# The RMS factor taken from the layer norm's variance, with memsets, routing steps, filler products and gathers re-placed, in an image tower with mixture-of-experts on one core

## The chip, the core and the metric

The kernel runs on one NeuronCore of a Trainium2 chip, with everything in float32. The metric is device time in microseconds: the median of several executions of one launch. Engine names are those of the profile: PE is TensorE (PEld its weight loads), DVE VectorE, ACT ScalarE, POOL GpSimd, SP SyncE.

## What is computed

32 images are cut into 25 patches each and embedded; with the class token that is 26 tokens of 192 numbers per image, 832 in all. Then come a first causal attention (12 heads of 16), and a block of a second causal attention (12 query heads of 64 on 3 key heads, with rotary turns) and 16 experts of which each token uses 2. Cut to what matters for the change:

```python
def _layernorm(x, eps=1e-5):
    m, v = mean(x), var(x)
    return (x - m) / sqrt(v + eps)

def rms_norm(x, w):                       # EPS = 1e-6
    return x / sqrt(mean(x * x) + EPS) * w

h = tok(x, W, b)                          # patches, bias, position; class token in front
h = h + attn1(_layernorm(h))
z = _layernorm(h)                         # input of the block, and its residual
x2 = z + attention2(rms_norm(z, norm1_w))
h = h + x2 + moe(rms_norm(x2, norm2_w))   # router, softmax, top 2 of 16, silu(gate) * up, down
```

`z` has mean 0 and mean square v / (v + 1e-5). So the factor of the first `rms_norm` can be had from v alone: (h - m) times 1 / sqrt(v (1 + 1e-6) + 1e-6 * 1e-5).

## The kernel before

**Tiles and stages.** A tile holds 4 images (32 rows each, 26 used), a group two tiles; there are 4 groups. Each group goes through stage A (patches, first attention, residual `h`, layer norm `z`, product input `u`) and stage B (second attention, `x2`, norm, router logits), in eight phases each, `a1` to `a8` and `b1` to `b8`. The function `stages` sets the order by hand, the same for all engines: two stages run as a pair, phase by phase. The pairs are A0 with A1, B0 with A2, B1 with A3, B2 with B3. Every engine executes its part of each phase in that order, and the engines meet by semaphores. The routing steps of the first four tiles (`choose`, `ranks`, `place`, `scatter`) are hung into the last pair, after the phase of B2 that the last argument of `stages` names; those of the other four tiles follow the pair.

**End of stage A (`a8`).** DVE adds the projection to the residual (L893), takes mean and variance of the rows (`layer_stats`: L799, L803), adds epsilon (L806). POOL raises to -0.5 (`rstd`, L516). DVE writes `zB` (`normalise`, L811). ACT squares it and sums (`squares`, L674), DVE scales the sum (`mean_square`, L818), POOL raises again (L516), DVE writes `u` (L899). PE transposes `u` (`turned`, L1089), ACT copies the result out of the bank with the norm's weight (L689).

**Start of stage B.** PE makes value products (L1216) and rotary ones (L1228); DVE multiplies those by the turn table (L912), POOL adds the halves (L555) and spreads the keys (L560). PE may make the fourth rotary set when DVE has read the first, since they share a bank. POOL's `pads` zeroes four buffers (L507 to L510) in `b1` of groups 0 and 3.

**Filler.** `keep_busy` (L1100) issues products that nobody reads ahead of a wait of PE.

**End of stage B.** Output products (L1286) give `x2` on DVE (L948), ACT squares it (L674), DVE scales (L818), POOL raises (L516) and adds the residual (L570), DVE writes `u` (L951), SP stores it as the experts' input, PE transposes it and makes the logits (L1301).

**Routing.** `choose` (L974 to L987) takes the two best experts, `place` (L994 to L1013) numbers the slots, and POOL's `scatter` writes 4 tiles times 2 choices into the slot table by eight indirect DMAs (L580). After the last of all 16, SP reads 28 tile entries one after the other (L462), and after these issues the later half of the late expert weights (L358).

**Experts.** A tile of 128 slots is gathered (L596), transposed (L1328), multiplied by one expert's gate and up weights (L1333), gated (L762, L1053), transposed (L1341), multiplied by the down weights (L1350), scaled (L1057) and scattered to its token's row (L602). Between 13 and 28 tiles can be used; POOL runs 8 gathers ahead, and each `step` issues one scatter and one gather. At the end both parts and the residual are added and stored.

## Time and profile before

| | us |
|---|---|
| median of 3 runs (336.48 to 338.42) | 337.66 |
| the profiled execution | 340.81 |
| its span | 338.9 |
| busy: PE | 274.5 (81%) |
| busy: DVE | 149.4 (44%) |
| busy: POOL | 123.8 (37%) |
| busy: ACT | 91.5 (27%) |

The mean granted clock of TensorE was 0.934 of full speed. A tenths digit of the page stands for 8.5 us of the span. PE's busy time holds filler products: 376 recorded rows of L1100, 48.4 us. Each matmul of the program shows as two recorded rows (20 rotary products of a group are x40 in the trace). A wait is put down to the event that came last; the busy shares are means over stages with different limits.

### The profile page before, as it was taken

How to read it: one execution, taken by the hardware profiler on the slowest of the kernel's cores; microseconds unless marked ns; L12 is line 12 of the kernel's file. 1: busy time of each engine (PE TensorE's matmuls, PEld its weight loads, DVE VectorE, ACT ScalarE, POOL GpSimd, SP SyncE). 2: the span in 40 equal slices, each digit the busy share in tenths (PEclk: the TensorE clock that was granted, in tenths of full speed). 3: DMA queues.
4: the chain of work that ended last, by engine and by line, in shares of the span. 5: the costliest groups of instructions: out<-in, count | busy, mean ns of one | idle time of the engine just before them, and what ended most of it. 6: DMA issues, size and time to landing. Idle time of an engine off the chain costs nothing.

```text
span 338.9 us, 5708 instructions
## 1 busy us (share of the span) xinstructions
PE 274.5 (81%) x1917; PEld 232.9 (69%) x1917; DVE 149.4 (44%) x347; ACT 91.5 (27%) x248; POOL 123.8 (37%) x138
## 2 busy tenths in 40 slices
PE   1999889979889999698999779803899999999900
PEld 0988779868768889487998669703677776777600
DVE  0143845764744568733867843570022222222204
ACT  1016640204532216512100532100233333333200
POOL 5030002573001291011794056063334523666640
PEclk9999999959999999999999999755899999999965
DMA  7301992004500007000000000392111596222226
GB/s 297 156 2 43 390 314 71 2 0 140 140 0 21 0 2 186 2 5 17 1 2 0 3 1 21 96 343 76 37 35 39 163 281 169 72 70 58 62 72 219
DMA packets 16641, 30.56 MB, mean 90 GB/s; under 512 B 6500, under 2 KB 10820, under 8 KB 15780
## 3 DMA queue, kind: packets, MB, share of 16 engines
q1 hardware_dynamic: 11140, 20.43, 20.1%
q0 software_dynamic: 2720, 4.55, 4.8%
q10 hardware_dynamic: 2752, 5.18, 4.5%
q8 instruction: 20, 0.33, 0.4%
q14 instruction: 9, 0.07, 0.1%
HBM read 26.07 MB, written 4.09 MB: 89 GB/s over the span
## 4 chain that ended last, share of the span: by engine, by line
PE 31%; DVE 21%; issue 16%; POOL 14%; DMA 11%; ACT 6%; SPq 0%; POOLq 0%; DVEq 0%; ACTq 0%
PE bank L1228 8%; POOL front L596 4%; POOL slots L580 4%; DMA experts<-wgu 4%; POOL parts L602 3%; PE bank L1244 3%; PE bank L1286 2%; PE bank L1333 2%; POOL rstd_a L516 2%; PE bank L1112 2%; DVE experts L835 2%; DMA front<-fw 2%; DVE experts L951 2%; DMA front<-moe_in,probs_by_key 2%; DVE experts L829 2%
## 5 line engine op out<-in xcount | busy, mean ns | idle before, releaser
L1100 PE MATMUL bank<-constants 128*128 128x96 f32 x376 | 48.4, 289 | 15.3 <-DMA slots<-slot_contents,slot_index 15.3
L1100 PEld LDWEIGHTS bank<-constants 128*128 128x128 f32 x376 | 47.1, 205 | 16.0 <-DMA slots<-slot_contents,slot_index 15.5
L1333 PE MATMUL bank<-experts,probs_by_key 96*128 x152 | 52.3, 487 | 0.6 <-ACT probs_by_key L758 0.6
L596 POOL DMA_INDIRECT front<-moe_in,probs_by_key x27 | 25.9, 958 | 44.8 <-DMA front<-moe_in,probs_by_key 40.1
L1333 PEld LDWEIGHTS bank<-experts,probs_by_key 96*128 96x128 f32 x152 | 27.3, 190 | 16.0 <-issue 0.8
L1053 DVE TENSOR_TENSOR probs_by_key<-bank,probs_by_key 128x384 f32<-128x384 f32 x19 | 10.6, 558 | 59.7 <-PE bank L1333 59.7
L1228 PE MATMUL bank<-experts,front 96*96 96x208 f32 x160 | 31.8, 360 | 2.4 <-DVE experts L912 2.4
L516 POOL TENSOR_TENSOR rstd_a<-variance_a,constants 128x2 f32<-128x2 f32 x12 | 8.3, 694 | 69.6 <-DVE variance_a L806 62.2
L1228 PEld LDWEIGHTS bank<-experts,front 96*96 96x96 f32 x160 | 27.8, 174 | 5.5 <-DVE experts L912 2.8
L580 POOL DMA_INDIRECT slots<-slot_contents,slot_index x16 | 16.1, 1009 | 28.9 <-DVE slot_index L1013 24.6
L912 DVE TENSOR_TENSOR experts<-bank,constants 96x416 f32<-96x416 f32 x40 | 21.1, 580 | 10.8 <-POOL experts L555 10.1
L555 POOL TENSOR_TENSOR experts<-experts 96x416 f32<-96x416 f32 x20 | 21.0, 1067 | 6.3 <-DVE experts L912 6.2
L1350 PE MATMUL bank<-experts,probs_by_key 128*128 x114 | 21.7, 327 | 0.7 <-ACT probs_by_key L766 0.7
L602 POOL DMA_INDIRECT parts<-front,probs_by_key x19 | 18.8, 989 | 5.8 <-issue 4.9
L516 POOL TENSOR_TENSOR rstd_b<-variance_b,constants 128x2 f32<-128x2 f32 x4 | 2.8, 710 | 45.9 <-DVE variance_b L818 45.9
L1350 PEld LDWEIGHTS bank<-experts,probs_by_key 128*128 128x128 f32 x114 | 18.0, 190 | 0.9 <-issue 0.9
L758 ACT ACTIVATE probs_by_key<-bank 96x256 f32<-96x256 f32 x20 | 7.6, 379 | 40.9 <-PE bank L1328 40.9
L869 DVE TENSOR_TENSOR experts<-experts,constants 96x1248 f32<-96x1248 f32 x8 | 12.9, 1652 | 10.1 <-ACT experts L641 10.1
L1057 DVE TENSOR_SCALAR front<-bank,probs_by_key 128x192 f32 (+1 forms) x19 | 7.9, 418 | 17.4 <-PE bank L1350 17.4
L1112 PE MATMUL bank<-front,patches 128*128 128x192 f32 x72 | 15.0, 376 | 0.5 <-DVE embedding_base L846 0.5
L674 ACT ACTIVATE experts<-experts 128x192 f32<-128x192 f32 x16 | 5.7, 358 | 36.0 <-DVE experts L811 19.3
L1112 PEld LDWEIGHTS bank<-front,patches 128*128 128x128 f32 x72 | 14.4, 226 | 1.0 <-DVE embedding_base L846 1.0
(167 smaller groups left out, 442.3 us busy)
## 6 DMA issues: line engine op xcount, KB each, us to landing
experts<-wgu SPq DMA_DIRECT2D x6, 768.0 KB, 8.9
experts<-wgu SPq DMA_DIRECT2D x12, 288.0 KB, 8.8
patches<-xp SPq DMA_DIRECT2D x6, 384.0 KB, 3.8
experts<-wdn SPq DMA_DIRECT2D x1, 2304.0 KB, 16.4
experts<-wdn ACTq DMA_DIRECT2D x8, 288.0 KB, 4.3
front<-fw SPq DMA_DIRECT2D x1, 1840.0 KB, 9.5
experts<-wgu ACTq DMA_DIRECT2D x4, 288.0 KB, 6.6
front<-fw SPq DMA_DIRECT2D x1, 776.0 KB, 8.8
```

What stands on the lines that cost most here:

```text
L516: pool.tensor_tensor(rs[s][:, :], ve[s][:, :], const("neghalf"), ALU.pow).then_inc(rs_ready[n], 1)
L555: pool.tensor_tensor(to, w.tmp[:, n % 2, :, 0], w.tmp[:, n % 2, :, 1], ALU.add).then_inc(rope_add, 1)
L580: pool.indirect_dma_start(slots, bass.IndirectOffsetOnAxis(sidx[:, k, t:t + 1], 0), pay[:, k, t, :], None).then_inc(scattered, 16)
L596: pool.indirect_dma_start(xy[:, j * D:j * D + D], None, moe_in, bass.IndirectOffsetOnAxis(entry[:, j * 3 + 1:j * 3 + 2].bitcast(I32), 0)). ...
L602: pool.indirect_dma_start(parts, bass.IndirectOffsetOnAxis(entry[:, j * 3 + 2:j * 3 + 3].bitcast(I32), 0), xy[:, j * D:j * D + D], None).t ...
L869: last = dve.tensor_tensor(w.kbd[:, c], w.k1[:, c].unsqueeze(2).to_broadcast([C, GI, HC, S]), const("head_of_row", C).unsqueeze(1).unsquee ...
L912: last = dve.tensor_tensor(w.tmp[:, n % 2, m], eo, turn[:, m].unsqueeze(2).to_broadcast([C, 2, GI, S]), ALU.mult)
L1100: mm(bank[:, 0:96], eye, eye[:, 0:96], start=True, stop=True)
L1112: last = mm(w.ps[0][:, D * t:D * t + D], patches(n)[:, 128 * k:128 * k + 128], wpatch[:, k, :], start=(k == 0), stop=(k == PK - 1))
L1228: last = mm(w.ps[(2, 3, 0)[n % 3]][0:C, CT * e:CT * e + CT], wqk2[:, k, (n + 4) % 5, e, :], real(w.fTb, k), start=(k == 0), stop=(k == 1))
L1333: last = mm(ps[2 * half][:, 0:FF], xT[:, 128 * k:128 * k + 128], big[0:C, bass.ds(e * (4 * FF) + (GU0 + 2 * FF * k + FF * half), FF)], sta ...
L1350: last = mm(ps[5][:, 0:D], hT[:, 128 * k:128 * k + 128], big[:, bass.ds(e * (3 * D) + D * k, D)], start=(k == 0), stop=(k == 2))
```

## The change

1. `layer_stats` makes for the second layer norm a second variance column pair, v (1 + 1e-6) + 1e-11, beside the first, and POOL raises all four columns at once. DVE writes `u` straight from the residual, and `zB` after it. The squares on ACT, the scaling on DVE and the second power of `a8` are gone. What ACT waited for in `a8` of groups 2 and 3 (the stored tokens and the transpose of the group two before, which read the same buffer) DVE waits for now.
2. The four memsets of group 0's stage B move from `b1` to `a3` of group 1 (three) and `a6` of group 0 (one). Those of group 3 stay.
3. `place` goes from after phase 4 to after phase 5 of B2, the first `scatter` from after phase 4 to after phase 7.
4. Filler: in `b1` from 18, 0, 18, 0 to 9, 0, 10, 0 products for groups 0 to 3; in `b7` from 7, 7, 4, 11 to 7, 7, 0, 11.
5. From tile 13 on, a step of POOL gathers only if the tile number reached is not past the count of used tiles.

```diff
@@ -511,9 +511,10 @@
-                s = (0, 0, 0, 1)[n]
+                s, cols = ((0, GT), (0, 2 * GT), None, (1, GT))[n]
                 pool.wait_ge(ve_ready[n], g + 1)
-                pool.tensor_tensor(rs[s][:, :], ve[s][:, :], const("neghalf"), ALU.pow).then_inc(rs_ready[n], 1)
+                pool.tensor_tensor(rs[s][:, 0:cols], ve[s][:, 0:cols], const("neghalf")[:, 0:cols], ALU.pow)\
+                    .then_inc(rs_ready[n], 1)
@@ -527,10 +528,23 @@
+            def a3(g):
+                if g == 1:
+
+                    pool.memset(B[0].p2[:, :, :, :, S:32], 0.0)
+                    pool.wait_ge(patch_done, 4)
+                    pool.memset(B[0].ot2a, 0.0)
+                    pool.memset(B[0].ot2b, 0.0)
+
+            def a6(g):
+                if g == 0:
+
+                    pool.wait_ge(o_done, 1)
+                    pool.memset(B[0].pbd, 0.0).then_inc(pads_set, 1)
+
             def a8(g):
                 rstd(g, 1)
-                rstd(g, 2)
@@ -539,11 +553,6 @@
                     pool.wait_ge(u_ready[0], GROUPS)
-                    pads(B[g])
-                elif g == 0:
-
-                    pool.wait_ge(o_done, 1)
-                    pool.wait_ge(patch_done, 4)
                     pads(B[g])
@@ -580,8 +589,8 @@
-            stages([a1, a2, nothing, nothing, nothing, nothing, nothing, a8],
-                   [b1, b2, nothing, nothing, nothing, b6, nothing, nothing], {4: scatter})
+            stages([a1, a2, a3, nothing, nothing, a6, nothing, a8],
+                   [b1, b2, nothing, nothing, nothing, b6, nothing, nothing], {7: scatter})
             scatter(1)
@@ -605,8 +614,13 @@
                 if j + AHEAD < STEPS:
-                    pool.wait_ge(gathered, (j + AHEAD) * 16)
-                    gather(j + AHEAD)
+                    if j < FEWEST:
+                        pool.wait_ge(gathered, (j + AHEAD) * 16)
+                        gather(j + AHEAD)
+                    else:
+                        with pool.If(used >= j + AHEAD):
+                            pool.wait_ge(gathered, (j + AHEAD) * 16)
+                            gather(j + AHEAD)
@@ -667,21 +681,6 @@
-            def squares(w, s, ready):
-
-                for t in range(GT):
-                    act.wait_ge(*ready(t))
-                    act.activation(w.u[:, t, :], w.zB[:, t, :], ACT.Square,
-                                   accum_out=ms[s][:, t:t + 1]).then_inc(sq_ready[s], 1)
-
-            def a8(g):
-                w = A[g]
-                if g >= 2:
-
-                    act.wait_ge(tokens_out[g % 2], 16 * IPT)
-                    act.wait_ge(mt_done, g - 1)
-                squares(w, 0, lambda t: (z_ready[1], g + 1))
-
             def b1(g):
@@ -741,7 +743,7 @@
-            stages([nothing, a2, a3, a4, a5, nothing, a7, a8], [b1, b2, b3, b4, b5, b6, b7, nothing],
+            stages([nothing, a2, a3, a4, a5, nothing, a7, nothing], [b1, b2, b3, b4, b5, b6, b7, nothing],
                    {1: gate_exp, 2: copy_ranks})
@@ -803,21 +805,18 @@
                 dve.wait_ge(mom_ready[n], g + 1)
-                dve.tensor_scalar(ve[0][:, :], mom[:, :, 1], LN_EPS, None, ALU.add).then_inc(ve_ready[n], 1)
-
-            def normalise(g, n, src, to):
+                last = dve.tensor_scalar(ve[0][:, 0:GT], mom[:, :, 1], LN_EPS, None, ALU.add)
+                if n:
+                    last = dve.tensor_scalar(ve[0][:, GT:2 * GT], mom[:, :, 1], 1.0 + RMS_EPS, RMS_EPS * LN_EPS,
+                                             ALU.mult, ALU.add)
+                last.then_inc(ve_ready[n], 1)
                 dve.wait_ge(rs_ready[n], g + 1)
-                for t in range(GT):
-                    last = dve.tensor_scalar(to[:, t, :], src[:, t, :], mom[:, t, 0:1], rs[0][:, t:t + 1],
+
+            def normalise(src, to, first, ready):
+                for t in range(GT):
+                    last = dve.tensor_scalar(to[:, t, :], src[:, t, :], mom[:, t, 0:1], rs[0][:, first + t:first + t + 1],
                                              ALU.subtract, ALU.mult)
-                last.then_inc(z_ready[n], 1)
-
-            def mean_square(g, n):
-                s = n - 2
-                dve.wait_ge(sq_ready[s], g * GT + GT)
-                dve.tensor_scalar(ve[s][:, :], ms[s][:, :], 1.0 / D, RMS_EPS, ALU.mult, ALU.add)\
-                   .then_inc(ve_ready[n], 1)
-                dve.wait_ge(rs_ready[n], g + 1)
+                last.then_inc(ready, 1)
@@ -893,11 +892,12 @@
                 layer_stats(g, 1, w.hB, h1_ready)
-                normalise(g, 1, w.hB, w.zB)
-                mean_square(g, 2)
-                for t in range(GT):
-                    last = dve.tensor_scalar(w.u[:, t, :], w.zB[:, t, :], rs[0][:, t:t + 1], None, ALU.mult)
-                last.then_inc(u_ready[0], 1)
+                if g >= 2:
+
+                    dve.wait_ge(tokens_out[g % 2], 16 * IPT)
+                    dve.wait_ge(mt_done, g - 1)
+                normalise(w.hB, w.u, GT, u_ready[0])
+                normalise(w.hB, w.zB, 0, z_ready[1])
@@ -946,7 +946,9 @@
                     dve.tensor_tensor(w.zB[:, t, :], w.ps[(3, 0)[t]][:, 0:D], w.zB[:, t, :], ALU.add).then_inc(x2_ready, 1)
-                mean_square(g, 3)
+                dve.wait_ge(sq_ready, g * GT + GT)
+                dve.tensor_scalar(ve[1][:, :], ms[:, :], 1.0 / D, RMS_EPS, ALU.mult, ALU.add).then_inc(ve_ready[3], 1)
+                dve.wait_ge(rs_ready[3], g + 1)
                 for t in range(GT):
@@ -1015,7 +1017,7 @@
             stages([a1, nothing, a3, a4, nothing, a6, nothing, a8], [nothing, b2, b3, b4, b5, b6, nothing, b8],
-                   {1: choose, 4: place})
+                   {1: choose, 5: place})
             choose(1)
@@ -1203,7 +1205,7 @@
                 w = B[g]
-                keep_busy(w.ps[0], (18, 0, 18, 0)[g])
+                keep_busy(w.ps[0], (9, 0, 10, 0)[g])
                 pe.wait_ge(u_ready[0], g + 1)
@@ -1289,7 +1291,7 @@
                 w = B[g]
-                keep_busy(w.ps[1], (7, 7, 4, 11)[g])
+                keep_busy(w.ps[1], (7, 7, 0, 11)[g])
                 pe.wait_ge(u_ready[1], g + 1)
```

The width of `neghalf`, of `variance_a` and of `rstd_a` doubles; `meansq_a` and one semaphore are gone.

Names in the rows below: `rstd_a` and `variance_a` are the factor and variance of the layer norms, `rstd_b` and `variance_b` those of the second RMS norm; `experts`, `front`, `patches`, `probs_by_key` and `attended` are large buffers reused for the stages' tiles; what stands in brackets is what the instruction waits for. On DVE, the end of stage A of one group (`a8`), before:

```order
L806 TENSOR_SCALAR variance_a<-moments 128x2 [waits mom_ready_b]
L811 TENSOR_SCALAR experts<-experts,moments,rstd_a 128x192 [waits rs_ready_1]
L811 TENSOR_SCALAR experts<-experts,moments,rstd_a 128x192
L818 TENSOR_SCALAR variance_a<-meansq_a 128x2 [waits sq_ready_a]
L899 TENSOR_SCALAR experts<-experts,rstd_a 128x192 [waits rs_ready_2]
L899 TENSOR_SCALAR experts<-experts,rstd_a 128x192
```

and now:

```order
L808 TENSOR_SCALAR variance_a<-moments 128x2 [waits mom_ready_b]
L810 TENSOR_SCALAR variance_a<-moments 128x2
L817 TENSOR_SCALAR experts<-experts,moments,rstd_a 128x192 [waits rs_ready_1]
L817 TENSOR_SCALAR experts<-experts,moments,rstd_a 128x192 x3
```

One wait for POOL is left of two, and the wait for ACT is gone; of the last four, two write `u` and two `zB`. On POOL, from the first stage A to the rotary adds of group 0, before:

```order
L528 TENSOR_TENSOR experts<-experts,front 128x384 [waits z_ready_a]
L516 TENSOR_TENSOR rstd_a<-variance_a,constants 128x2 [waits ve_ready_1]
L516 TENSOR_TENSOR rstd_a<-variance_a,constants 128x2 [waits ve_ready_2]
L516 TENSOR_TENSOR rstd_a<-variance_a,constants 128x2 [waits ve_ready_1]
L516 TENSOR_TENSOR rstd_a<-variance_a,constants 128x2 [waits ve_ready_2]
L507 MEMSET probs 104x24x6 [waits patch_done,o_done]
L508 MEMSET attended 128x1024
L509 MEMSET attended 128x512
L510 MEMSET probs_by_key 128x2496
L516 TENSOR_TENSOR rstd_a<-variance_a,constants 128x2 [waits ve_ready_0]
L555 TENSOR_TENSOR experts<-experts 96x416 [waits rope_mul]
```

and now:

```order
L529 TENSOR_TENSOR experts<-experts,front 128x384 [waits z_ready_a]
L534 MEMSET probs 104x24x6
L536 MEMSET attended 128x1024 [waits patch_done]
L537 MEMSET attended 128x512
L543 MEMSET probs_by_key 128x2496 [waits o_done]
L516 TENSOR_TENSOR rstd_a<-variance_a,constants 128x4 [waits ve_ready_1] x2
L516 TENSOR_TENSOR rstd_a<-variance_a,constants 128x2 [waits ve_ready_0]
L564 TENSOR_TENSOR experts<-experts 96x416 [waits rope_mul]
```

The memsets stand ahead of the powers of `a8` instead of behind them. On POOL, from the last rotary adds of groups 2 and 3 to the end of the slot scatters, the difference is:

```order
-L580 DMA slots<-slot_contents,slot_index 14848x3 [waits gates_set,idx_ready,fill_set,filled]
-L580 DMA slots<-slot_contents,slot_index 14848x3 x7
...
-L580 DMA slots<-slot_contents,slot_index 14848x3 [waits gates_set,idx_ready,fill_set,filled]
-L580 DMA slots<-slot_contents,slot_index 14848x3 x7
...
+L589 DMA slots<-slot_contents,slot_index 14848x3 [waits gates_set,idx_ready,fill_set,filled]
+L589 DMA slots<-slot_contents,slot_index 14848x3 x7
+L589 DMA slots<-slot_contents,slot_index 14848x3 [waits gates_set,idx_ready,fill_set,filled]
+L589 DMA slots<-slot_contents,slot_index 14848x3 x7
```

Before, the two powers and the two residual adds of `b6` stood between the first eight scatters and the second; now all sixteen follow them.

## Rows read from the trace of the kernel before

**Rows 1.** The page, the chain that ended last, by engine.

```profile
PE 31%; DVE 21%; issue 16%; POOL 14%; DMA 11%; ACT 6%; SPq 0%; POOLq 0%; DVEq 0%; ACTq 0%
```

**Rows 2.** Timeline, 51 to 62 us: start, length, engine, line, tiles, count, idle before.

```profile
53.12 0.70 POOL L516 TENSOR_TENSOR rstd_a<-variance_a,constants 128x2 f32<-128x2 f32 x1 [28.44 <-DVE variance_a L806]
53.86 0.67 DVE L811 TENSOR_SCALAR experts<-experts,moments,rstd_a 128x192 f32<-128x192 f32 x2 [0.81 <-POOL rstd_a L516]
...
56.37 0.55 DVE L899 TENSOR_SCALAR experts<-experts,rstd_a 128x192 f32<-128x192 f32 x2 [0.80 <-POOL rstd_a L516]
...
57.45 4.07 PE L1112 MATMUL bank<-front,patches 128*128 128x192 f32 x24
...
61.69 1.54 PE L1216 MATMUL bank<-front,experts 96*128 96x192 f32 x8 [0.18 <-ACT experts L689]
```

**Rows 3.** Timeline, 61 to 76 us: memsets, held instruction, first rotary products of group 0.

```profile
61.83 3.71 DVE L899 TENSOR_SCALAR experts<-experts,rstd_a 128x192 f32<-128x192 f32 x1 [0.80 <-POOL rstd_a L516]
...
63.25 2.18 POOL L510 MEMSET probs_by_key<- 128x2496 f32 x1
...
65.69 0.55 DVE L858 TENSOR_TENSOR experts<-bank,embedding_base 128x384 f32<-128x384 f32 x1
...
68.76 2.07 DVE L912 TENSOR_TENSOR experts<-bank,constants 96x416 f32<-96x416 f32 x4
69.89 5.86 PE L1228 MATMUL bank<-experts,front 96*96 96x208 f32 x16 [2.44 <-DVE experts L912]
...
75.55 0.70 PE L1089 MATMUL bank<-constants,experts 128*96 128x128 f32 x3
```

**Rows 4.** Timeline, 113 to 123 us: the same products of group 1.

```profile
113.79 1.54 PE L1216 MATMUL bank<-front,experts 96*128 96x192 f32 x8 [0.75 <-ACT experts L689]
...
115.17 7.20 PE L1228 MATMUL bank<-experts,front 96*96 96x208 f32 x40
```

**Rows 5.** Timeline, 160 to 168 us: DVE in the pair of groups 2 and 3.

```profile
160.36 0.55 DVE L899 TENSOR_SCALAR experts<-experts,rstd_a 128x192 f32<-128x192 f32 x2 [0.80 <-POOL rstd_a L516]
...
162.04 2.73 DVE L981 TENSOR_SCALAR topf<-topi,constants 128x8 f32<-128x8 uint32 x1
...
165.27 2.08 DVE L912 TENSOR_TENSOR experts<-bank,constants 96x416 f32<-96x416 f32 x4
```

**Rows 6.** Timeline, 197 to 208 us: attention products, output products, third power.

```profile
197.74 1.62 PE L1269 MATMUL bank<-front,experts 128*64 128x416 f32 x8 [1.87 <-DVE front L935]
...
204.00 4.06 PE L1286 MATMUL bank<-front,patches 128*128 128x192 f32 x24
...
205.08 0.17 DVE L818 TENSOR_SCALAR variance_b<-meansq_b 128x2 f32<-128x2 f32 x1 [0.52 <-ACT experts L674]
...
207.12 0.74 POOL L516 TENSOR_TENSOR rstd_b<-variance_b,constants 128x2 f32<-128x2 f32 x1
```

**Rows 7.** Timeline, 211 to 233 us: POOL's last residual add and slot scatters.

```profile
211.44 1.01 POOL L570 TENSOR_TENSOR residual<-experts 128x384 f32<-128x384 f32 x1
...
222.30 1.04 POOL L580 DMA_INDIRECT slots<-slot_contents,slot_index  x1 [9.85 <-DVE slot_index L1013]
...
225.29 1.03 POOL L580 DMA_INDIRECT slots<-slot_contents,slot_index  x1 [0.30 <-issue]
...
231.68 0.95 POOL L580 DMA_INDIRECT slots<-slot_contents,slot_index  x1 [0.31 <-issue]
```

**Rows 8.** The page's gathers; the timeline, 320 to 325; the chain's last scatter.

```profile
L596 POOL DMA_INDIRECT front<-moe_in,probs_by_key x27 | 25.9, 958 | 44.8 <-DMA front<-moe_in,probs_by_key 40.1
...
322.28 0.42 DVE L1057 TENSOR_SCALAR front<-bank,probs_by_key 128x192 f32 x1 [1.81 <-PE bank L1350]
...
325.36 3.34 DMA parts<-front,probs_by_key
```

**Rows 9.** Who waited for whom: line, waited for, us in all, times, longest.

```profile
ACT experts L674 <- DVE experts L811: 19.3, 4, 5.2
```

**Rows 10.** Busy time by stretch: us, PE, PEld, DVE, ACT, POOL busy (count), PEclk, DMA.

```profile
69.90:76.00 6.10, 6.10 (x19) 4.98 (x20) 3.31 (x7) 0.00 (x0) 5.76 (x6) 0.50 0.00 0
```

18 lines of the change are left out of this document (10 added, 8 removed).

## The prediction

> **What bounds the kernel now.** I read the chain of waits first. No engine owns it: PE has 31%, DVE 21%, issue 16%, POOL 14%, DMA 11%, ACT 6% [rows 1]. So a microsecond is worth a microsecond only where it lies on the chain, and the timeline has to say where. Five stretches matter.
>
> *The end of stage A.* One token group goes from POOL's first power (53.12) through DVE's normalise (53.86 to 54.53), two squares on ACT and a second power to the product `u`, done at 56.92 [rows 2]. PE takes the next patches only after it (57.45). Its value products start at 61.69, released by ACT's copy of the turned `u`: ACT had to do the squares of the second group first [rows 2].
>
> *The first memsets.* The first `u` instruction of the second group is a 0.3 us job and lasts 3.71 us, from 61.83 [rows 3]. POOL's four memsets run beside it, the last from 63.25 to 65.43; DVE comes free when they end, not when the first does. The next group's add starts at 65.69 and the first rotary product at 68.76, so PE sits idle before 69.89 and does 16 rows in 5.86 us, where 40 rows take 7.20 us elsewhere [rows 3, 4].
>
> *Group 1 of stage B* differs from it only by the 0.75 us that PE waits for ACT at 113.79 [rows 4].
>
> *The pair of groups 2 and 3* has the same train of memsets; here a tiny scalar instruction lasts 2.73 us [rows 5].
>
> *Routing.* Placement on DVE, then eight scatters on POOL, stand ahead of work of the chain: PE idles 1.87 us before 197.74, and the third power, whose input was there at 205.25, starts at 207.12 behind the scatters [rows 6]. In the experts' tail POOL issues a gather for each scatter; the last scatter starts at 325.36, though its tile was scaled at 322.70 [rows 8].
>
> **The change, part by part.** Times are of the profiled execution: 338.9 us of span, 340.81 us in all, 3.15 above the median of 337.66. I take savings from either alike.
>
> *A, the end of stage A with the memsets, up to PE's transposes at 75.55.* The added variance instruction costs at most 0.17 us, like the small one at 205.08 [rows 6]; I take 0.1. The power now has four columns. No row shows that. Its low end is the 0.70 us of two [rows 2], its high end twice that, +0.70; an ordinary POOL add of 384 columns takes 1.01 us [rows 7], so columns as such are nearly free and only the power itself may cost. I take +0.25. Then `u` of group 0 is ready at 53.12 + 0.1 + 0.25 + 0.74 + 0.67 = 54.9 instead of 56.9. The patches end 2.05 us earlier, at 59.5 instead of 61.5. PE goes straight on, since ACT has no squares: the rotary rows start 1.38 us after the value products, as in group 1 (113.79 to 115.17), 40 of them take 7.20 us [rows 4], and the next transposes start 0.2 us before their end, as at 75.55 now [rows 3]: 67.8. DVE must keep up. Its second group follows by four instructions of 0.3 us each and the same chain, and is through at 59.6; the next add is then at 59.6 (was 65.69) and the first rotary product 3.07 us later, at 62.7, against PE's first result at 62.3 and its fourth set, which needs that product, at 65.2. So PE runs without a stop. **A = 75.55 - 67.8 = 7.75 us**, 7.3 to 8.0 with the ends of the power's price.
>
> The memsets themselves cost nothing at their new places: three run early in stage A, while DVE waits for ACT's copies of the keys, the large one beside PE's last attention products and DVE's scaling out of a bank, well before the next power at 53.12. If that cover went, it would be the 2.18 us of the large one [rows 3].
>
> *B, group 1.* The 0.75 us at 113.79 go: ACT copies at once, and PE's patches are next in line. **B = 0.75.** PE is the bound there, so the 2 us of the shorter factor are worth no more.
>
> *C, groups 2 and 3.* `u` of group 3 is ready 2.1 us earlier by the same chain, at 158.8 instead of 160.91 [rows 5], and ten filler products in place of 18 leave room for it. But its end releases the second train of memsets while DVE still has two normalise instructions for `zB`. Who gets in? The held instructions of rows 3 and 5 show that an engine that is in with a queue of work keeps the other out. `zB`'s first is already running when POOL asks, so I let DVE finish, and the memsets, 3.7 us, then hold the scalar instruction at 162.04 as now. With 0.6 us for `zB`, 3.7 for the memsets and 0.5 from the held instruction's end to the first rotary product (164.77 to 165.27 [rows 5]) that comes at 158.8 + 4.8 = 163.6: 1.67 earlier, and the 0.25 us that the softmax waited for PE's second tile go too. **C = 1.9**, 0.75 if POOL wins.
>
> The Trainium skill ("SBUF — State Buffer", Who interferes with whom) has such an instruction blocked until the instruction that holds the pair finishes. By that rule the instruction at 61.83 would have been let in after the first, short memset, and about 3.3 us of A would not be there to win. The trace disagrees: 3.71 us, through three further memsets; the sum goes by the trace.
>
> *D, routing up to the last slot scatter.* Placement moves behind the next group's copies: PE's 1.87 us [rows 6] go, and placement holds DVE's next attention copy for about 1 us, while PE has 4.1 us of the other group's output products to make [rows 6]: hidden. The third power is no longer behind scatters: 205.33 - 1.87 = 203.46. For group 3, PE's rows end at 208.06 - 1.87, the variance follows 0.91 us later as it did for group 2 [rows 6], the power at 207.35, the residual add ends at 209.05 instead of 212.45: 3.4 us. Now sixteen scatters stand in one train. At the undisturbed interval of 1.26 us the sixteenth starts 18.9 us later, at 227.95; between 222.30 and 225.29 two intervals took 2.99 us instead of 2.52 beside DVE's work [rows 7]. The second eight were 0.56 slower in all, and I give the first eight, beside the other half of choosing and placing, half of that: 228.8 against 231.68. **D = 2.9**, 2.6 to 3.2.
>
> *From there to the experts' tail* everything hangs on the last scatter: SP's entries, the gathers, and the late weights, which SP issues behind its entries. All move together. Value: 0.
>
> *E, the tail.* Nineteen tiles are used, so the gathers of numbers 21 to 26 (27 now, 21 then) are skipped from the fourteenth tile on [rows 8]. The last scatter follows its tile at 322.8 instead of 325.36. The scatter before it starts at its own tile too, over 2 us earlier. **E = 2.55.** An inner branch is added per step; it would have to cost 0.9 us to count.
>
> The wait for stored tokens and for the transpose of the group two before moves from ACT to DVE, where `u`, `zB` and everything behind queue up. Today ACT's squares wait for it at the same place, and all four idles before them were ended by DVE's normalise, not by a store [rows 9]. Value 0; if a store came late, all of its delay would count.
>
> Filler products removed: they only filled waits that shrink. Value 0.
>
> Sum: 7.75 + 0.75 + 1.9 + 2.9 + 2.55 = **15.85 us**; 337.66 - 15.85 = **321.8 us** (profiled 325.0).
>
> **Rivals.**
> 1. *POOL's memsets win over `zB`.* For it: POOL won each meeting in the trace; against: it was in first each time. DVE is held 3.7 us with five instructions still ahead, PE stalls about 1 us, C = 0.75: **322.9**. Chance 0.15.
> 2. *The train of scatters becomes the bound.* All sixteen at the slow interval (1.50): 15 x 0.24 = 3.6 us, less 0.8 counted: **324.6**. For it: rows 7; against: the eight scatters from 197.03 kept 1.26 beside DVE copies. Chance 0.13. The Trainium skill ("SBUF — State Buffer", SBUF: two separate sides) says that DVE's two-port instructions lock POOL out of writing descriptors; that speaks against this move.
> 3. *The skip does not pay*: a taken inner branch costs as much as the gather did. E = 0 to 1.3, **324.3** or a little above. Chance 0.07.
> 4. *Slower than before: the clock.* Half of the filler in stages B0 and B2 is gone. If PE falls to the lower level (1.2 GHz) there and stays down for the products behind it, each PE microsecond costs a second one. Before, 69.90 to 76.00 ran at 0.50 after an idle of 2.44 us [rows 3, 10]. In B0 4.07 + 1.54 + 7.20 = 12.8 us of PE work stand behind the filler, in groups 2 and 3 twice 1.54 + 7.20 = 17.5: 321.8 + 30.3 = **352.1** if both run low throughout. It decides from 17.5 us of PE work at the low level. Against it: the idles left are 0.2 to 0.7 us. Chance 0.02.
>
> **How the numbers follow.** Forecast 0.61, rivals 0.15, 0.13, 0.07 and 0.02, anything else 0.02. The predicted time is the forecast's. Low end: the cheap power (+0.5), D and a faster last landing (+1.2), and a run-to-run spread of 1 us give 319, and I allow one more: 318. High end: rivals 2 and 3 together 327. 0.5% (1.7 us) is about what a measurement of this kernel can tell from no change. Faster by more than that: 0.95; within: 0.02; slower: 0.03, the clock and what I have not seen.
>
> **What would show it.** Right: no DVE instruction of 3.71 us near 60; PE's 40 rotary rows of the first B group in one run at full clock; the power of four columns near 0.95 us; the third power at once after its variance; sixteen scatters in a row, each about 1.26 apart; 21 gathers; last scatter 0.1 us after its tile. Wrong: a long normalise instruction on `zB` beside the later memsets (rival 1), intervals of 1.5 (rival 2), 1 us gaps between POOL's last scatters (rival 3), PEclk below 9 in the slices from 55 to 80 us (rival 4). A late weight wait of more than 1 us in the experts would overthrow "all move together".

## The result and the profile after

The change takes 325.87 us (median of 4 runs, 325.02 to 327.10) where before takes 337.64 (4 runs, 336.48 to 338.42): ratio 0.9657, 95% interval 0.9613 to 0.9700. In a later comparison it took 327.16 us (6 runs, 326.43 to 328.32) to 338.77 (11 runs): 0.9693, 0.9645 to 0.9742. The saving is 11.6 to 11.8 us at the medians; 15.85 were forecast. Medians and ranges hold all executions, ratios leave out those over 1.5% above the fastest of their kernel; a saving that stands beside a ratio comes from the ratio, and can be smaller than the difference of the medians. The profiled execution after has a span of 324.4 us and 326.30 in all.

The page after, PE's granted clock in 40 slices, the chain that ended last, and four groups (busy us, mean ns; idle before them and what ended it):

```profile
PEclk9999999999999999899997899855999999999985
...
PE 47%; POOL 15%; DVE 15%; issue 11%; DMA 5%; ACT 5%; SPq 1%; POOLq 0%; DVEq 0%; ACTq 0%
...
L605 POOL DMA_INDIRECT front<-moe_in,probs_by_key x21 | 20.1, 957 | 37.9 <-DMA front<-moe_in,probs_by_key 32.5
...
L611 POOL DMA_INDIRECT parts<-front,probs_by_key x19 | 18.7, 982 | 14.6 <-DVE front L1059 10.3
...
L589 POOL DMA_INDIRECT slots<-slot_contents,slot_index x16 | 15.9, 994 | 4.8 <-issue 4.8
```

PE's share of the chain rises from 31% [rows 1] to 47%, and 21 gathers are left of 27 [rows 8]. In the 22nd and 23rd slice (170 to 187 us) the clock line dips to 7 and 8: that is new, and the second profile has it too (6 and 7). The 8 of the 17th slice (130 to 138 us) is in this profile alone.

The timeline after, 52 to 76 us, answers to rows 2 and 3 (start, length, engine, line, operation, tiles, count, idle before):

```profile
52.51 1.02 POOL L516 TENSOR_TENSOR rstd_a<-variance_a,constants 128x4 f32<-128x4 f32 x1 [3.91 <-DVE variance_a L810]
...
57.61 1.25 DVE L817 TENSOR_SCALAR experts<-experts,moments,rstd_a 128x192 f32<-128x192 f32 x4 [1.12 <-POOL rstd_a L516]
58.87 0.56 DVE L857 TENSOR_TENSOR experts<-bank,embedding_base 128x384 f32<-128x384 f32 x1
...
58.67 1.47 PE L1218 MATMUL bank<-front,experts 96*128 96x192 f32 x8
59.97 7.20 PE L1230 MATMUL bank<-experts,front 96*96 96x208 f32 x40
67.01 0.60 PE L1091 MATMUL bank<-constants,experts 128*96 128x128 f32 x4
```

DVE's instructions are not held, and PE does not stop in the rotary products: forty rows in one run, transposes at 67.01 instead of 75.55 [rows 3]. The power of four columns takes 1.02 us.

The pair of groups 2 and 3 after, 148 to 187 us; it answers to rows 5 and 6:

```profile
148.49 4.70 DVE L817 TENSOR_SCALAR experts<-experts,moments,rstd_a 128x192 f32<-128x192 f32 x4 [1.13 <-POOL rstd_a L516]
...
149.30 0.30 POOL L507 MEMSET experts<- 104x144 f32 x1 [0.85 <-DVE experts L817]
...
150.90 2.17 POOL L510 MEMSET front<- 128x2496 f32 x1
...
155.05 2.07 DVE L912 TENSOR_TENSOR experts<-bank,constants 96x416 f32<-96x416 f32 x4
...
156.18 3.05 PE L1230 MATMUL bank<-experts,front 96*96 96x208 f32 x16 [0.81 <-DVE experts L912]
...
172.25 4.68 PE L1246 MATMUL bank<-experts 96*104 96x78 f32 x32 [1.32 <-POOL experts L564]
176.72 1.94 PE L1102 MATMUL bank<-constants 128*128 128x96 f32 x8
...
179.50 4.39 PE L1102 MATMUL bank<-constants 128*128 128x96 f32 x34
183.73 0.70 PE L1259 MATMUL bank<-constants,experts 104*128 104x104 f32 x6
```

Four `u` and `zB` instructions of 0.3 us each take 4.70: the last of them begins beside the first memset and comes free with the fourth. PE stops for 0.81 us, then for 1.32 before the scores of group 3 (172.25). While it makes those, its clock falls to the lower level (1.2 GHz): the granted clock is 0.64 of full speed over them and 0.50 behind them. 32 rows take 4.68 us that take 3.07 elsewhere, then 8 filler rows 1.94 that take 1.07. That, and the 34 filler rows behind, make the transposes of group 3 start at 183.73, though DVE had the probabilities at 181.98.

Routing after; it answers to rows 6 and 7:

```profile
193.80 0.17 DVE L950 TENSOR_SCALAR variance_b<-meansq_b 128x2 f32<-128x2 f32 x1 [0.52 <-ACT experts L729]
194.05 0.70 POOL L516 TENSOR_TENSOR rstd_b<-variance_b,constants 128x2 f32<-128x2 f32 x1 [21.85 <-DVE variance_b L950]
...
199.83 1.23 POOL L589 DMA_INDIRECT slots<-slot_contents,slot_index  x1 [0.19 <-issue]
...
219.36 0.95 POOL L589 DMA_INDIRECT slots<-slot_contents,slot_index  x1 [0.30 <-issue]
```

The third power follows its variance at once, and sixteen scatters run in one train.

The tail after:

```profile
309.88 0.42 DVE L1059 TENSOR_SCALAR front<-bank,probs_by_key 128x192 f32 x1 [1.81 <-PE bank L1352]
...
310.58 0.95 POOL L611 DMA_INDIRECT parts<-front,probs_by_key  x1 [1.27 <-DVE front L1059]
```

The last scatter starts 0.28 us after its tile is done, where 0.1 was forecast; before it was 2.7 [rows 8].

To see where time goes I cut profiled executions at eight events: second set of patch products, first rotary product of group 0, first scores product, third power (`rstd_b` of group 2), last slot scatter, first gather, last tile scaled, last scatter. Each column is the length up to its event from the one before, all from start to start, in us:

| kernel | patches | rotary | scores | third power | last slot scatter | first gather | last tile | last scatter | end | span |
|---|---|---|---|---|---|---|---|---|---|---|
| before | 15.67 | 47.40 | 18.48 | 125.57 | 24.56 | 5.69 | 84.91 | 3.08 | 13.54 | 338.9 |
| before, second profile | 14.29 | 47.39 | 17.19 | 125.61 | 24.64 | 5.70 | 84.33 | 4.34 | 12.61 | 336.1 |
| forecast | 15.67 | 45.21 | 12.92 | 119.26 | 25.34 | 5.69 | 84.91 | 0.53 | 13.54 | 323.1 |
| the change | 14.99 | 44.98 | 12.83 | 121.25 | 25.31 | 6.33 | 84.19 | 0.70 | 13.82 | 324.4 |
| the change, second profile | 14.49 | 44.98 | 12.83 | 122.81 | 25.64 | 7.24 | 84.14 | 0.69 | 12.38 | 325.2 |

The forecast's row is the first one less A (2.19 + 5.56), less B, C and the 3.66 of the third power (0.75 + 1.9 + 3.66), with D's longer train (+0.78), less E (2.55). The second and fourth columns of before repeat to 0.05 us, so what moves there is the change. The fourth stands out: 6.31 us were to be won there, and 4.32 and 2.76 were. In span the first profile of the change is only 1.3 us above the forecast's row (324.4 to 323.1). That is luck in part: its patches and its experts (columns one and seven), for which nothing was forecast, are 0.7 us each below those of the profile that the forecast started from.

### The profile page after: what moved, and what is told of

Read it like the earlier page. It is cut to its first block, busy times and chain, and to the rows that moved or that the text cites. A ratio compares the mean times of both kernels' runs of the same rounds, so it can differ in the third digit from the quotient of the medians.

```text
span 324.4 us, 5597 instructions
## 1 busy us (share of the span) xinstructions
PE 268.3 (83%) x1875; PEld 227.8 (70%) x1875; DVE 147.8 (46%) x347; ACT 88.5 (27%) x232; POOL 117.8 (36%) x128
## 4 chain that ended last, share of the span: by engine, by line
PE 47%; POOL 15%; DVE 15%; issue 11%; DMA 5%; ACT 5%; SPq 1%; POOLq 0%; DVEq 0%; ACTq 0%
PE bank L1335 9%; PE bank L1230 4%; PE bank L1114 4%; PE bank L1102 4%; PE bank L1288 4%; POOL slots L589 4%; POOL parts L611 3%; PE bank L1246 3%; PE bank L1352 3%; POOL experts L564 3%; DVE experts L817 2%; POOL front L605 2%; DMA front<-fw 2%; PE bank L1271 2%; DMA attended<-parts 2%
## 5 line engine op out<-in xcount | busy, mean ns | idle before, releaser
L1102 PE MATMUL bank<-constants 128*128 128x96 f32 x334 | 44.1, 293 | 16.7 <-DMA slots<-slot_contents,slot_index 16.7
L1102 PEld LDWEIGHTS bank<-constants 128*128 128x128 f32 x334 | 42.9, 209 | 17.3 <-DMA slots<-slot_contents,slot_index 16.8
L605 POOL DMA_INDIRECT front<-moe_in,probs_by_key x21 | 20.1, 957 | 37.9 <-DMA front<-moe_in,probs_by_key 32.5
L1230 PE MATMUL bank<-experts,front 96*96 96x208 f32 x160 | 29.0, 339 | 0.8 <-DVE experts L912 0.8
L1230 PEld LDWEIGHTS bank<-experts,front 96*96 96x96 f32 x160 | 26.0, 163 | 3.1 <-DVE experts L912 1.2
L516 POOL TENSOR_TENSOR rstd_a<-variance_a,constants 128x2 f32<-128x2 f32 (+1 forms) x8 | 6.9, 859 | 39.8 <-DVE variance_a L808 20.1
L868 DVE TENSOR_TENSOR experts<-experts,constants 96x1248 f32<-96x1248 f32 x8 | 14.0, 1786 | 8.5 <-ACT experts L655 8.5
L817 DVE TENSOR_SCALAR experts<-experts,moments,rstd_a 128x192 f32<-128x192 f32 x24 | 11.8, 546 | 7.8 <-POOL rstd_a L516 7.8
L1246 PE MATMUL bank<-experts 96*104 96x78 f32 x128 | 13.9, 274 | 1.3 <-POOL experts L564 1.3
L1246 PEld LDWEIGHTS bank<-experts 96*104 96x104 f32 x128 | 13.7, 189 | 1.7 <-POOL experts L564 1.5
```

Of the source, the lines that this page charges most:

```text
L605: pool.indirect_dma_start(xy[:, j * D:j * D + D], None, moe_in, bass.IndirectOffsetOnAxis(entry[:, j * 3 + 1:j * 3 + 2].bitcast(I32), 0)). ...
L817: last = dve.tensor_scalar(to[:, t, :], src[:, t, :], mom[:, t, 0:1], rs[0][:, first + t:first + t + 1], ALU.subtract, ALU.mult)
L868: last = dve.tensor_tensor(w.kbd[:, c], w.k1[:, c].unsqueeze(2).to_broadcast([C, GI, HC, S]), const("head_of_row", C).unsqueeze(1).unsquee ...
L1102: mm(bank[:, 0:96], eye, eye[:, 0:96], start=True, stop=True)
L1230: last = mm(w.ps[(2, 3, 0)[n % 3]][0:C, CT * e:CT * e + CT], wqk2[:, k, (n + 4) % 5, e, :], real(w.fTb, k), start=(k == 0), stop=(k == 1))
L1246: last = mm(w.ps[t][0:104, G * S * i:G * S * (i + 1)], w.qr[:, e, IPT * t + i].rearrange("p r q -> p (r q)"), w.kbd2[:, e, IPT * t + i].re ...
```

## The experiments

### The kernel before, once more

> The kernel before, unchanged, once more. Two theories of the 4.1 us missing from the forecast (15.85 us forecast, 11.8 us measured). P, the profiled execution of before was a slow one: its 340.81 us stood 3.15 us above the median of its timed runs, and a part of what its trace seemed to lose is lost only there. Then this profile ends nearer 337.7 us (span about 335.7), and some of the checkpoints come earlier than in the first: first normalise of h1(3) at 155.25, rotary transposes of group 0 at 75.55, third power at 207.12, last slot scatter at 231.68, last scatter at 325.36, end of span 338.9. The place where the new trace is ahead is where the 3 us were. I, interaction: the parts of the change take back from each other in groups 2 and 3; then this profile looks as the first, within 0.5 us at each checkpoint. Time in both: ratio 1.000, within 0.003.

Measured: 337.05 us (12 runs, 335.64 to 341.83) to 337.95 (28 runs, 333.86 to 341.13), ratio 1.0013 (0.9970 to 1.0055). Its profile, 336.1 us of span, and that of the next kernel, where nothing is changed at this place either, have the wait of 2.45 us of rows 3, and behind it stretches at the lower clock of different lengths. Before, second profile, 61 to 79 us:

```profile
68.50 4.66 PE L1228 MATMUL bank<-experts,front 96*96 96x208 f32 x16 [2.45 <-DVE experts L912]
72.96 0.72 PE L1089 MATMUL bank<-constants,experts 128*96 128x128 f32 x4
```

The kernel with the gathers alone, same place:

```profile
69.09 4.12 PE L1233 MATMUL bank<-experts,front 96*96 96x208 f32 x16 [2.45 <-DVE experts L917]
...
74.74 3.09 PE L1136 MATMUL bank<-experts,front 96*96 96x208 f32 x8 [0.68 <-ACT experts L637]
77.62 2.77 PE L1141 MATMUL bank<-front,experts 96*128 96x192 f32 x8
```

Sixteen rows take 5.86, 4.66 or 4.12 us; in the last case the low clock comes later and stays to the products at 77.62, which take 2.77 us instead of 1.46. In the table's third column that is 18.48, 17.19 and 20.13 us. So this stretch is drawn anew in each execution, and rows 3 were neither cheap nor dear: the four profiles with that wait unchanged average 18.6. Of the 2.8 us between the two profiles of before 1.4 lie ahead of the second patches, 1.3 here. Theory P is right that an execution of before can be 3 us above another, and the two profiles of before differ in the third column, which term A used. But A's part of it, 18.48, is the average of such executions; columns two and four repeat; what else differs (columns one, seven, eight and the end) is 1.4, 0.6, -1.3 and 0.9 us, and of these only the eighth, with 3.08 where the second profile has 4.34, entered a term, E, on the low side. P doesn't explain what is missing in column four.

### The parts alone

Four kernels, each before with one part of the change; lines are those of the diff above.

> Before, with the last six gathers left out alone (part 5 of the change). By the traces 2.55 us (2.36 to 2.66): the last scatter follows its tile by 0.3 us instead of 2.7. Ratio 0.9925. If an inner branch cost as much as a gather, 0 to 1.3 us, ratio 0.996 to 1. If the final loads of the residual parts are limited by something else than the scatter's landing (in the changed kernel they landed in pieces that were waited for), less than 2 us.

Measured: 334.22 us (11 runs), ratio 0.9916 (0.9880 to 0.9952): 2.8 us, where 2.55 was forecast. The last scatter follows its tile by 0.69 us in its profile, counted from start to start, against 3.08 and 4.34 in the two of before.

> Before, with place and the first eight scatters moved as in part 3 of the change, nothing else. By the traces 2.9 us (ratio 0.9914): the third power at once after its variance (1.87 us), sixteen scatters in one train at 1.30 us each. Theory I (interaction in groups 2 and 3) also says 2.9 here, since nothing else is changed; theory P (a slow profile of before) says that part of it is not there: 2 us or less.

Measured: 336.06 us (12 runs), ratio 0.9954 (0.9920 to 0.9988): 1.55 us, interval 0.4 to 2.7. In its profile the fourth column is 121.73 (before 125.57) and the fifth 25.37 (before 24.56): 3.0 us together. The profile's 3.0 lies just above the interval of the times.

> Before, with the four memsets of group 0 at the places of part 2 of the change, nothing else. Without the train, u of group 0's second tile is done by 62.1, the next add follows at 62.4, the first rotary product at about 65.5, PE's rotary rows start 1.4 us after the value products at 63.1 and run on without or with a short stop: transposes at 70.1 to 70.5 instead of 75.55. 5.3 us, ratio 0.984. By the rule that a held instruction is let in when the memset that holds it ends, about 3.3 us of that would not be there: 2 us, ratio 0.994. By theory P something between.

Measured: 332.34 us (6 runs, 331.42 to 334.10), ratio 0.9870 (0.9823 to 0.9918): 4.4 us, 2.8 to 6.0. The wait and the low clock are gone from its profile:

```profile
62.79 7.20 PE L1237 MATMUL bank<-experts,front 96*96 96x208 f32 x40
```

The third column falls to 12.82 us. Its 6 runs spread over 2.7 us, the 28 of before over 7.3.

> Before, with part 1 alone (one power of four columns, u straight from the residual; memsets, routing, filler and gathers as before). Where parts 1 and 2 work on the same wait, the train of memsets now follows the second group's power directly and still holds DVE: the next add comes 2 to 3 us earlier than 65.69, first rotary product near 66, transposes of group 0 near 72.8. B 0.75, C at most 1. If the parts are additive in this way: 3.5 to 4.6 us, ratio 0.988. The rival: without part 2 the memsets meet more of DVE's instructions, and PE's 36 filler instructions (4.16 us) end after u is there, so that the shorter chain is hidden: 0 to 2 us, ratio 0.997.

Measured: 332.35 us (6 runs, 329.42 to 334.95) to 336.96 (11 runs), ratio 0.9856 (0.9806 to 0.9907): 4.9 us, 3.1 to 6.5. The second column falls by 1.05 us, the third to 14.31, the fourth to 124.02. In its profile the train of memsets meets the four instructions of the second group, and PE waits 0.61 us instead of 2.45, at full clock:

```profile
58.21 4.58 DVE L803 TENSOR_SCALAR experts<-experts,moments,rstd_a 128x192 f32<-128x192 f32 x4 [1.12 <-POOL rstd_a L516]
...
66.92 3.06 PE L1216 MATMUL bank<-experts,front 96*96 96x208 f32 x16 [0.61 <-DVE experts L898]
...
175.69 3.16 PE L1232 MATMUL bank<-experts 96*104 96x78 f32 x32 [1.08 <-POOL experts L555]
```

The four ratios give 2.8 + 1.55 + 4.4 + 4.9 = 13.65 us, each with over a microsecond of uncertainty. Parts 1 and 2 work on the same wait: in columns two and three together part 1 wins 5.3 us from the average of before, part 2 5.7, and both 8.2. The sum of the parts counts about 2.8 us there twice; the forecast had worked A out as a whole. Part 4, the filler, was not taken alone; the next experiment takes it out of the change.

### Filler as before

```diff
-                keep_busy(w.ps[0], (9, 0, 10, 0)[g])
+                keep_busy(w.ps[0], (18, 0, 18, 0)[g])
-                keep_busy(w.ps[1], (7, 7, 0, 11)[g])
+                keep_busy(w.ps[1], (7, 7, 4, 11)[g])
```

> The change with the filler counts of before. By the change's trace filler of 2.15 us (18 products before 54.29) becomes 4.2: PE's transposes of u come 1.5 us later in group 0, and PE is the bound behind them; in groups 2 and 3 the filler before 147.49 grows by 1.9 us where PE idles 1.12 in any case: 0.8 us. 2.0 to 2.5 us slower than the change, near 328. The rival (less filler is what lets PE fall to the lower clock at the scores of group 3, 172.25 to 179): the half-clock stretch goes, 2.5 us back: no difference, near 326.

Measured: 329.87 us (6 runs, 326.96 to 330.35), ratio to before 0.9795 (0.9749 to 0.9841). The ratio is 0.0138 above that of the change in its first comparison and 0.0102 above the later one, 4.7 and 3.4 us; the kernel of the next experiment, measured beside this one, is 4.3 us faster. So the old counts cost more than the 2.0 to 2.5 expected. More filler does not keep the clock up at the scores of group 3 either:

```profile
173.74 5.69 PE L1246 MATMUL bank<-experts 96*104 96x78 f32 x32 [1.08 <-POOL experts L564]
```

Part 4, costed at nothing, is a condition of A and C: without it PE's 4.16 us of filler (18 products, 36 rows) end after `u` is there. The same 1.08 us of idleness stood ahead of full clock in the kernel with the factor alone. So the length of this wait does not by itself decide the clock.

### Who goes first, memsets or `zB`

```diff
-                    pool.wait_ge(u_ready[0], GROUPS)
+                    pool.wait_ge(z_ready[1], GROUPS)
```

> The change, with POOL's four memsets of group 3 released by the end of zB instead of by the end of u. This is the order that the forecast took for groups 2 and 3. zB then takes 0.6 us instead of 4.1, the memsets run at about 149.8 to 153.6 and hold one of DVE's small selection instructions. If I was right about C but for who gets in, the first rotary product comes about 1.1 us earlier (154.0 instead of 155.05) and the time falls by 0.6 to 1.2 us, ratio to the change 0.997. Rival: any memset behind u holds DVE as long as it runs, so nothing changes: 325.9.

Measured: 325.55 us (6 runs, 324.35 to 326.95), ratio to before 0.9679 (0.9640 to 0.9718): not told apart from the change. The profile shows the order that the forecast had assumed:

```profile
148.57 1.25 DVE L817 TENSOR_SCALAR experts<-experts,moments,rstd_a 128x192 f32<-128x192 f32 x4 [1.13 <-POOL rstd_a L516]
...
150.96 2.73 DVE L983 TENSOR_SCALAR topf<-topi,constants 128x8 f32<-128x8 uint32 x1
...
154.19 2.07 DVE L912 TENSOR_TENSOR experts<-bank,constants 96x416 f32<-96x416 f32 x4
...
171.38 3.69 PE L1246 MATMUL bank<-experts 96*104 96x78 f32 x32 [1.31 <-POOL experts L564]
```

The first rotary product comes at 154.19 instead of 155.05 and PE's 0.81 us wait is gone, but the 1.31 us one and the low clock stay. The fourth column is 120.25 us, 1.0 and 2.6 less than in the two profiles of the change, though the times do not show it; the order was not the whole of what C lacked.

### The memsets of group 3 taken apart

`pbd` of group 3 lies over the weights of stage A. `EARLY` is 2304: up to that column the weights below it are no longer read once the attention of stage A is done.

```diff
             def pads(w):
 
                 pool.memset(w.p2[:, :, :, :, S:32], 0.0)
-                pool.memset(w.ot2a, 0.0)
-                pool.memset(w.ot2b, 0.0)
-                pool.memset(w.pbd, 0.0).then_inc(pads_set, 1)
+                pool.memset(w.keyed[:, EARLY:G * GT * CT * 2], 0.0).then_inc(pads_set, 1)
...
             def a3(g):
...
+                elif g == 3:
+
+                    pool.wait_ge(patch_done, TILES)
+                    pool.memset(B[3].ot2a, 0.0)
+                    pool.memset(B[3].ot2b, 0.0)
 
             def a6(g):
...
+                elif g == 3:
+
+                    pool.wait_ge(o_done, GROUPS)
+                    pool.memset(B[3].keyed[:, 0:EARLY], 0.0)
```

> The change, with group 3's memsets taken apart: the 1024 and 512 columns beside the stage before (behind the last patches), 2304 of the 2496 columns behind the last attention products of stage A; only 144 and 192 columns stay behind u. If the meeting of the memsets and zB is what cost C (and the half clock at the scores of group 3 follows from PE's 1.32 us wait for POOL's rotary adds, which run without a pause from 156.21 to 172.2), then zB takes under 1.2 us, the first rotary product comes at about 152, POOL's adds end 3 us earlier, the scores of group 3 run at full clock (3.1 us instead of 4.7), and the transposes of group 3 at 183.73 come 2.5 to 3.1 us earlier: 2.5 to 3 us faster than the change, near 323.1. Rival: POOL's adds or the softmax on DVE bound this stretch in any case: under 1 us.

Measured: 323.01 us (6 runs, 322.05 to 324.43), ratio to before 0.9608 (0.9568 to 0.9647), in one comparison with the kernel above (325.55). Most steps come as expected:

```profile
148.83 1.42 DVE L826 TENSOR_SCALAR experts<-experts,moments,rstd_a 128x192 f32<-128x192 f32 x4 [1.14 <-POOL rstd_a L516]
...
152.94 1.08 DVE L921 TENSOR_TENSOR experts<-bank,constants 96x416 f32<-96x416 f32 x2 [0.75 <-PE bank L1239]
...
170.95 3.16 PE L1255 MATMUL bank<-experts 96*104 96x78 f32 x32 [0.72 <-POOL experts L573]
173.94 1.07 PE L1111 MATMUL bank<-constants 128*128 128x96 f32 x8
...
180.62 0.76 PE L1268 MATMUL bank<-constants,experts 104*128 104x104 f32 x6 [0.76 <-DVE experts L931]
```

DVE now waits for PE (0.75 us before the rotary product at 152.94, where 152 was expected), the scores of group 3 run at full clock, and the transposes start at 180.62, 3.1 us earlier. One step does not: POOL's last rotary add ends at 170.90, 1.3 us earlier than in the change and not 3, since POOL now waits for DVE and DVE for PE (0.77 us at 161.73). PE's wait before the scores is 0.72 us instead of 1.32. The fourth column falls to 118.64 us: 6.93 less than before, where 6.31 were forecast and the change won 4.32 and 2.76. So what column four lacked comes from the meeting of the memsets with `zB`, and what follows from it.

### Filler in the wait before the scores of group 3

```diff
             def b3(g):
                 w = B[g]
 
+                if g == 3:
+                    pe.wait_ge(v2_ready, g + 1)
+                    keep_busy(w.ps[1], 5)
                 pe.wait_ge(rope_add, g * 5 + 5)
```

> The change with 10 unread filler instructions (1.2 us) between the scores of group 2 and those of group 3, where PE waits 1.32 us for POOL's rotary adds. The wait stays, its idleness goes. If the clock fell because PE stood idle there, the scores of group 3 take 3.1 us instead of 4.7 and the filler behind 1.1 instead of 1.9; the transposes at 183.73 come when DVE's probabilities are there, at about 182.2: 1.5 us faster than the change, 324.4. If the clock falls for another cause (the load of the minute before), nothing changes, or it gets slower by up to 0.3 us.

Measured, beside the change in the same comparison (327.16 us, 326.43 to 328.32): 324.51 us (6 runs, 323.61 to 325.56): 2.65 us faster, and the runs do not overlap. POOL's adds end as late, but PE is idle for 0.15 us only:

```profile
171.57 1.29 PE L1102 MATMUL bank<-constants 128*128 128x96 f32 x10
173.02 3.16 PE L1249 MATMUL bank<-experts 96*104 96x78 f32 x32 [0.15 <-POOL experts L564]
176.01 1.07 PE L1102 MATMUL bank<-constants 128*128 128x96 f32 x8
...
182.47 0.76 PE L1262 MATMUL bank<-constants,experts 104*128 104x104 f32 x6 [0.76 <-DVE experts L922]
```

So in the change the fall of the clock follows from that idleness: with POOL's adds as late as before, the scores run at full clock. The fourth column is 120.01 us, 1.2 and 2.8 less than in the two profiles of the change; taking the memsets apart, which removes the late adds too, gives 2.6 and 4.2. The low clock is thus half to two thirds of the loss. The 1.5 us expected were read from the first profile of the change; in the second, taken beside this kernel, the low stretch is longer.

### The change, once more

> The changed kernel once more. If the half-clock stretch at the scores of group 3 belongs to the change (PE's 1.32 us wait before 172.25 brings it), it is in this profile too: 32 score products in 3.7 to 4.7 us instead of 3.1, 8 filler instructions in 1.9 instead of 1.1. If it was chance, as the length of the one near 70 us is in the kernel before, they run in 3.1 and 1.1 us and the span is 1.5 to 2.5 us shorter. Time: 325.9, and a narrower spread than before's (333.9 to 341.1 over 28 runs), since the wait near 70 us is gone: within 2.5 us from end to end.

Measured: 327.16 us (6 runs), spread 1.9 us. The low clock is there again and lasts longer: the granted clock is 0.59 over the scores and 0.50 from there to 182 us:

```profile
171.69 5.04 PE L1246 MATMUL bank<-experts 96*104 96x78 f32 x32 [1.29 <-POOL experts L564]
176.52 1.94 PE L1102 MATMUL bank<-constants 128*128 128x96 f32 x8
...
179.29 5.66 PE L1102 MATMUL bank<-constants 128*128 128x96 f32 x34
```

It belongs to the change; its length varies, and with it the fourth column (122.81 and 121.25).

### Routing back at its old place

The change with these:

```diff
-                   [b1, b2, nothing, nothing, nothing, b6, nothing, nothing], {7: scatter})
+                   [b1, b2, nothing, nothing, nothing, b6, nothing, nothing], {4: scatter})
...
-                   {1: choose, 5: place})
+                   {1: choose, 4: place})
```

> The change with place and the first scatters at their old places. Forecast D was 2.9 us; the part alone gave 1.5 us (0.4 to 2.7) in the times, 2.7 us in its trace between the first scores and the last slot scatter. By the traces: third power 3.7 us later against the first scores, last slot scatter 2.7 to 2.9 us later, time 328.7, ratio to the change 1.009. If the time says 1.5 us again, something behind the last scatter gives a part back.

Measured: 328.48 us (6 runs, 327.27 to 329.95) to 327.16: 1.3 us, not the 2.9 forecast. Its profile says why in part:

```profile
184.27 0.70 PE L1259 MATMUL bank<-constants,experts 104*128 104x104 f32 x6
...
187.97 1.62 PE L1271 MATMUL bank<-front,experts 128*64 128x416 f32 x8 [0.75 <-DVE front L935]
```

PE waits 0.75 us for the copies behind `place`, not the 1.87 of rows 6, since it comes late itself (184.27) out of the low clock. While C is lost, 1.1 us of D is not there to win: the wait for `place` hides that much of PE's lateness. Its fourth column is 123.93, against 121.25 and 122.81, its fifth 25.16.

### Keys of groups 2 and 3 on ACT

On top of the memsets taken apart:

```diff
-                    if n == 0:
+                    if n == 0 and g < 2:
...
+                if g >= 2:
+                    act.wait_ge(rope_add, g * 5 + 1)
+                    kr = w.kr.rearrange("p e i k -> p (e i) k")
+                    bd = w.kbd2.rearrange("p e i g k -> p (e i) g k")
+                    for n in range(G):
+                        last = act.activation(bd[:, :, n, :], kr, ACT.Copy, scale=const("group_of_row", C)[:, n:n + 1])
+                    last.then_inc(kbd2_ready, 1)
```

> The kernel with the early memsets of group 3 (early_pads), and the block-diagonal keys of groups 2 and 3 (POOL, two products of 2.47 us per group) made by ACT, which has no work there for 12 us: three scaled copies of 416 columns, 0.5 us each. If POOL's unbroken run of 16 us bounds the scores of group 3, its adds end 2.5 us earlier or more, PE's 0.72 us wait before 170.95 goes and DVE's first softmax starts by up to 1 us earlier, when the scores are there: 0.7 to 1.2 us faster than early_pads (323.0), 322.0. Rival: the softmax chain on DVE is bound by PE's scores, which move by 0.7 at most, and waits for the attended copies behind it: under 0.4 us.

Measured: 322.75 us (6 runs, 321.75 to 323.62), ratio to before 0.9559 (0.9511 to 0.9606), 4.4 us faster than the change in the same comparison. The 64 scores products of both groups run without a stop:

```profile
166.98 6.00 PE L1262 MATMUL bank<-experts 96*104 96x78 f32 x64
...
175.15 0.75 PE L1275 MATMUL bank<-constants,probs 104*128 104x104 f32 x6 [1.25 <-DVE probs L938]
```

PE then waits 1.25 us for DVE's softmax instead of 0.30, so that the fourth column is 118.66, as without this edit (118.64). The rival was right: the wait for POOL went, and DVE's chain, which starts with the scores of group 2, took its place. This kernel beats both before and the change in one comparison. The one without the keys' edit beats before, and the change by its ratio (0.9608 to 0.9657 and 0.9693, taken in separate comparisons); between the two the times do not decide.

## Why the prediction was right and wrong

The direction, most steps and the range (318 to 327) held, though the later comparison's 327.16 us lies just beyond its upper end; the time was 4 us too low. A, B, D and E work as told; two terms of the sum do not: C with what hangs on it, and in a small way the 0 behind the last slot scatter. Point by point:

- **A right.** 7.75 was forecast. Columns two and three fall by 8.1 us from the first profile and by 6.8 from the second; from the average of the four with that wait (47.4 and 18.6) it is 8.2. The four-column power costs 0.32 us more than the two-column one, against 0.25 taken. The early memsets cost no visible wait.
- **B right.** PE's wait is gone: 4.07 us of patches, then the values at once.
- **C, the failing step: "I let DVE finish", and the price of the other case.** Rival 1 came about: POOL won. But it was priced at 1.15 us, since I followed the held instruction to PE's wait (0.81, forecast 1) and no further. The loss went on: POOL's rotary adds of the two groups run almost without a break, so a late first product makes the scores of group 3 wait 1.32 us; PE falls to 1.2 GHz there; and transposes that should follow DVE's probabilities start 1.7 us after them. With B at its 0.75 and D at its 3.66, column four leaves C = -0.1 in the first profile and -1.65 in the second, against 1.9: a miss of 2.0 to 3.6 us, the largest part of the 4. Taking the memsets apart brings C to 2.5; filler in PE's wait alone, with POOL's adds as late as they were, brings back 1.2 and 2.8 of column four and 2.65 us of the time. The split between C and D is a choice of order. With `place` at its old place column four leaves C = 0.8 (the factor alone, 124.02) and 0.9 (the change with the old routing, 123.93, low clock and all), close to the 0.75 of rival 1: there PE waits for `place` in any case, and its lateness costs little. Only when D takes that wait away does the lateness reach the third power. The forecast added C and D as if neither touched the other.
- **D, mechanism right, its full price only where C is won.** Third power at once, sixteen scatters in a row, 15 intervals in 19.53 us: 1.30 each, where 18.9 plus 0.84 = 19.74 was worked out. Rival 2 did not come about: beside DVE's work three intervals took 1.34 to 1.40 us instead of 1.26 (in the second profile the longest is 1.73), so DVE's work delays the scatters by tenths and does not keep them from being issued. In the times D is worth 1.55 us alone and 1.3 taken back, in profiles 3.0 alone. 1.1 us of the difference in the change is the wait for `place` that PE's own lateness hides. The rest stays open, and so does why the part alone shows less in the times than in its profile.
- **"All move together, 0": a small miss.** From the last slot scatter to the first gather the change takes 6.33 and 7.24 us, both profiles of before 5.7: 0.6 to 1.5 us given back. The cause stays open: in the profiles of the other kernels the stretch takes 5.3 us (the old filler) to 7.5 us (`zB` first), and it is not tied to one part of the change.
- **E right.** 2.8 us alone, against 2.55. The gap between the last tile's scaling and its scatter differs from one profile to the next while 27 gathers are issued (3.08 and 4.34 us before, 4.23, 2.24 and 1.02 in the parts without the skip), so the 2.55 read from one of them was near by luck too; it is 0.70 whenever 21 are issued. Rival 3 fell.
- **"I take savings from either alike": sound in its terms.** See the first experiment.
- **Filler and rival 4.** Less filler was costed at nothing; A and C needed it. Nothing fell to 1.2 GHz where rival 4 looked (stages B0 and B2, first products); the clock fell in the scores of group 3, for a wait that the forecast did not have.

On the meeting of the two engines the Trainium skill ("SBUF — State Buffer", Who interferes with whom) says that whoever issues first has the shared ports for the whole instruction and the other is blocked. The prediction read this as letting the held instruction in when the memset that holds it ends. No run here agrees with that reading: a single `zB` instruction is held for 3.83 us, through four memsets, and the memsets alone are worth 4.4 us where that rule left 2. Groups of line 817 after (ns min/median/max; first and last start, us):

```profile
L817 DVE TENSOR_SCALAR experts<-experts,moments,rstd_a x24: 368/374/3825, 17.8 to 149.4; 128x192 f32<-128x192 f32 x24
```

## What to carry to other kernels

Follow a collision that remains past the first wait it makes, to the next engine that works without a break and to PE's clock behind it: here 1.15 us of forecast collision cost two to three times that. Cut the profiles of before and after at the same few events before blaming the execution that was profiled. Before two savings are added, ask whether the later one removes the wait in which the earlier one's loss was hidden, as D did with C's. A train of POOL memsets is best cut up and put where DVE is idle for want of something else, and where a wait on PE cannot go, some unread products inside it may be worth more than the wait.
